# The read-out steps of a chunk moved to every second group in a selective scan kernel

## The chip, the cores and the metric

The kernel runs on one core of a Trainium2 chip. The metric is the device time of one execution in microseconds (us), from three runs of the kernel before: 1214.02, 1214.25 and 1216.48, median 1214.25.

## The reference

Two sequences of 1024 tokens with 256 channels pass through four layers with residual adds, each behind a layer norm: a selective scan (state size 64), a mixture of eight experts with two chosen for each token, a linear attention with 16 heads, and a gated feed-forward layer. The change touches only the first:

```
delta = softplus(delta @ dt_proj_w.T + dt_proj_b);  A = -exp(A_log)
step:  dA = exp(dt * A);  h = dA * h + dt * b * x;  y = einsum('bdn,bn->bd', h, c)
out = (y + x * D_param) @ out_proj_w.T
```

Here c comes from a position modulo 64, so all chunks of 64 tokens in a sequence use the same 64 rows c.

## The kernel before

The scan stage cuts the 2048 tokens into 32 chunks of T = 64 tokens and the 128 pairs of a chunk into GROUPS = 8 groups of G = 16. A list written by `scan_schedule` (line 619) gives one order of work for all engines; each engine walks the list and does its own part. For every group number gi (chunk c = gi // 8, place j = gi % 8) the entry "stream" stands for this:

- TensorE waits until the scan of group gi - 2 is done (it writes the same half of the input banks), issues `unread[gi - 1]` products that nobody reads, then 16 products with the inputs of group gi (line 927), and then 16 products with the decay exponents of group gi + 2 (line 908).
- ScalarE copies the carry of group gi - 1 into its inputs (`hand_on`, line 1094) and takes the exponential of the decays of group gi + 1 (line 1086).
- GpSimd makes the carry of group gi from the last column of the chunk before (lines 1414 and 1420) and clears the first column of its decays (line 1423).
- VectorE runs the scan of group gi - 2 (LAG = 2; line 1256), one instruction over 128 x 1024 elements, which writes h.

h has room for HS = 4 half chunks, that is two chunks: the scans of chunk c write where chunk c - 2 stood. For this a scan waits:

```
if c >= 2:
    dve.wait_ge(sem("y"), c - 1)
```

The read-out y of a chunk (lines 933 to 948) multiplies h with the rows c on TensorE: four steps j = 0 to 3, each of four matmuls (output on 32 partitions, 512 columns) into bank 6. The last of the 16 raises the semaphore "y" by one. The constant `Y_STEPS` says which steps stand in which group, counted from LAG groups after the start of the next chunk: entry 0 is place 2. After the read-out, ScalarE copies bank 6 out ("y_out", place 1 of the chunk after the next), SP moves the rows ("y_sel", place 3), and for every second chunk a tile of 128 rows is turned on TensorE ("yT", lines 976 and 981, place 5 of odd chunks), multiplied with w_out ("proj", place 1 of even chunks) and added to the residual on VectorE ("resid", line 1280).

Between these, the list spreads the preparation of later tokens ("u_" steps: for TensorE the transposes u_turn, line 993, and u_tx, line 543, and the projections u_proj, lines 999 and 1002, and u_dt, line 1011) and the router ("tr", "mm", "rank"). Those that write bank 7 may open only at certain places (`opens`, line 625): from chunk 3 on these are 1 and 3 in odd chunks and 4 and 6 in even chunks. `unread_after` (line 736) counts the other TensorE work of a group by `PE_WORK` (a read-out step and the turn count 4 each) and gives 3 less that many unread products, never below zero; they are issued at the head of the next group's stream.

Of the kernel before, what the change touches and what calls it, by code (L numbers as in the profile page):

```python
# [559 lines left out]
ZEROS = 4  # L560
CT = P // T
Y_SEL = 16 * 4
Y_STEPS = ((0,), (1,), (), (2,), (), (3,))
PE_WORK = {"y": 4, "u_turn": 4, "u_proj": 6, "u_dt": 4, "u_tx": 4, "tr": 2, "yT": 4, "proj": 4}
Y_OUT, Y_PICK = 7, 9
TILE_END = ((4, 4, "yT"), (5, 5, "yt"), (8, 6, "proj"), (8, 6, "proj2"), (10, 8, "resid"))
# [52 lines left out]
def scan_schedule():  # L619
# [46 lines left out]
    for gi in range(TOTAL + LAG):  # L666
# [13 lines left out]
        c_read -= 1  # L680
        if 0 <= c_read < CHUNKS and step < len(Y_STEPS) and Y_STEPS[step]:
            yield ("y", c_read, Y_STEPS[step])
        for at, what in ((Y_OUT, "y_out"), (Y_PICK, "y_sel")):
# [27 lines left out]
    yield from ((name, b3) for name in NORM)  # L711
    for js in (js for js in Y_STEPS if js):
        yield ("y", CHUNKS - 1, js)
# [1601 lines left out]
```

## Time and profile before

| | us |
|---|---|
| median of three runs | 1214.25 |
| profiled execution | 1212.75 |
| its span | 1211.4 |
| VectorE busy | 767.2 (63%) |
| TensorE matmul busy | 1082.1 (89%) |
| ScalarE busy | 515.0 (43%) |

The span runs from the first to the last instruction of the profiled execution. Busy time is the time in which an engine worked on an instruction; time in brackets is its share of the span. In the rows below, "idle before" in square brackets is the time in which the engine stood idle in front of the group, with the instruction that ended it. A row with x12 merges twelve instructions.

### The profile page before, as it was taken

The page shows a single profiled execution, that of the slowest core. Times are in us where ns is not written, and L with a number is a line of the kernel's source. Part 1 is how long each engine was busy: PE and PEld are TensorE (multiplying, and loading weights), DVE is VectorE, ACT ScalarE, POOL GpSimd, SP SyncE. Part 2 cuts the span into 40 slices and gives each one's busy share as a digit, 9 for nine tenths or more (in the row PEclk, how much of TensorE's full clock was granted, in tenths as well). Part 3 has the DMA queues.
Part 4 walks back from the last instruction along what each step waited for, and adds up shares of the span by engine and source line. Part 5 has one row for each costly group of instructions (what it writes and reads, how often), then busy time and mean ns, then how long its engine had stood idle before and what let it go on. Part 6 is the DMA issues. An engine that isn't in the chain of part 4 may idle for free. (4 is left out here: it accounts for less than half of the span.)

```text
span 1211.4 us, 30173 instructions
## 1 busy us (share of the span) xinstructions
PE 1082.1 (89%) x12319; PEld 729.7 (60%) x12319; DVE 767.2 (63%) x890; ACT 515.0 (43%) x1328; POOL 324.0 (27%) x949
## 2 busy tenths in 40 slices
PE   3888888888888899888878999999999899999998
PEld 2655564555545555545544777788866666576465
DVE  5999999999999999999982122111111567242111
ACT  3777676676766767656631111111112212112110
POOL 5344444343345434443242011111111210000000
PEclk9999999999999999998997999999999999999999
DMA  6767747352353434424217723232110400000000
GB/s 162 164 156 182 172 106 196 63 108 75 66 128 92 101 81 75 111 68 67 47 49 260 275 102 105 75 109 105 55 48 22 140 1 1 1 18 9 9 18 18
DMA packets 183899, 110.11 MB, mean 91 GB/s; under 512 B 95517, under 2 KB 178336, under 8 KB 181408
## 3 DMA queue, kind: packets, MB, share of 16 engines
q1 hardware_dynamic: 178816, 98.65, 31.9%
q0 software_dynamic: 3456, 8.48, 2.0%
q8 instruction: 97, 1.59, 0.6%
q10 hardware_dynamic: 1488, 1.05, 0.4%
q14 instruction: 42, 0.34, 0.1%
HBM read 63.25 MB, written 43.90 MB: 88 GB/s over the span
## 5 line engine op out<-in xcount | busy, mean ns | idle before, releaser
L1256 DVE TENSOR_TENSOR_SCAN h<-decay,psum 128x1024 f32<-128x1024 f32 x256 | 566.2, 2266 | 18.5 <-ACT psum L1094 11.0
L1086 ACT ACTIVATE decay<-psum 128x512 f32<-128x512 f32 x512 | 278.2, 596 | 47.6 <-PE psum L908 44.5
L927 PEld LDWEIGHTS psum<-xdiag,bstat 128*128 128x128 bf16 x4096 | 148.4, 99 | 122.3 <-DVE h L1256 86.7
L927 PE MATMUL psum<-xdiag,bstat 128*128 128x64 bf16 x4096 | 166.4, 195 | 22.3 <-DVE h L1256 21.1
L943 PE MATMUL psum<-h,cstat 128*32 128x512 f32 x1024 | 138.0, 613 | 3.1 <-DVE h L1256 2.1
L1583 PE MATMUL psum<-shared,hid 128*128 128x256 f32 x640 | 139.7, 379 | 0.9 <-DVE hid L1662 0.9
L1571 PE MATMUL psum<-xdt,shared 128*128 128x320 f32 (+2 forms) x512 | 139.5, 433 | 0.8 <-ACT xdt L1634 0.8
L1583 PEld LDWEIGHTS psum<-shared,hid 128*128 128x128 f32 x640 | 120.9, 190 | 17.7 <-issue 1.7
L894 PE MATMUL psum<-shared 128*128 128x512 bf16 x262 | 74.4, 391 | 60.6 <-DVE h L1256 60.6
L1571 PEld LDWEIGHTS psum<-xdt,shared 128*128 128x128 f32 x512 | 92.3, 190 | 45.2 <-issue 15.3
L908 PE MATMUL psum<-rows,shared 32*128 32x64 bf16 x4096 | 105.9, 191 | 12.4 <-DMA rows<-parts_d 8.8
L1414 POOL TENSOR_TENSOR carry<-decay,h 128x16 f32<-128x16 f32 x240 | 58.0, 242 | 208.2 <-ACT decay L1086 206.2
L2192 PE MATMUL psum<-xt,wgu 128*128 128x512 f32 x256 | 110.6, 592 | 0.0
L1695 POOL DMA_INDIRECT picked_d<-eo,to x40 | 38.9, 972 | 255.3 <-ACT eo L1631 153.0
L1662 DVE TENSOR_SCALAR hid<-psum 128x320 f32<-128x320 f32 (+1 forms) x56 | 29.1, 520 | 103.8 <-PE psum L1571 103.8
L1094 ACT COPY psum<-carry 128x16 f32<-128x16 f32 x240 | 43.3, 180 | 118.8 <-PE psum L927 99.7
L908 PEld LDWEIGHTS psum<-rows,shared 32*128 32x128 bf16 x4096 | 75.2, 94 | 27.2 <-issue 11.1
L2192 PEld LDWEIGHTS psum<-xt,wgu 128*128 128x128 f32 x256 | 48.6, 190 | 59.7 <-issue 59.5
L1665 DVE TENSOR_SCALAR eo<-psum,gate 128x256 f32<-128x256 f32 x19 | 9.2, 484 | 112.9 <-PE psum L1583 107.2
L1628 ACT ACTIVATE hid<-psum 128x320 f32<-128x320 f32 (+2 forms) x72 | 30.2, 419 | 117.7 <-PE psum L1571 117.7
L1965 DVE TENSOR_TENSOR shared<-psum,sil 128x512 f32<-128x512 f32 x32 | 22.1, 690 | 86.0 <-PE psum L2192 86.0
L1420 POOL TENSOR_TENSOR carry<-carry,u 128x16 f32<-128x16 f32 x240 | 52.9, 220 | 84.2 <-ACT u L1123 67.7
(243 smaller groups left out, 1073.4 us busy)
## 6 DMA issues: line engine op xcount, KB each, us to landing
shared<-in_w SPq DMA_DIRECT2D x16, 1024.0 KB, 4.8
xdiag<-x_parts_d SPq DMA_DIRECT2D x124, 96.0 KB
rows<-parts_d SPq DMA_DIRECT2D x128, 48.0 KB
x_parts_d<-x_parts SPq DMA_DIRECT2D x14, 384.0 KB, 3.3
x_parts_d<-x_parts SPq DMA_DIRECT2D x21, 256.0 KB, 3.2
disp_d<-r_xl SPq DMA_DIRECT2D x4, 1305.0 KB, 8.6
xd<-disp_d SPq DMA_DIRECT2D x8, 652.5 KB, 6.3
picked_d<-r_xl SPq DMA_DIRECT2D x4, 1024.0 KB, 5.4
```

The costliest lines, as they stand in the source:

```text
L894: pe.q.matmul(bank, s["astat"][:, 0, :], s["astat"][:, 0:4, :].rearrange("p c m -> p (c m)"), start=True, stop=True)
L908: ins = pe.q.matmul(bank_a[half][:, i * T:(i + 1) * T], s["astat"][strip, RCH * g + q, :], rows[strip, c % 2, q, :], start=True, stop=True)
L927: ins = pe.q.matmul(to.rearrange("p d (s e) -> p s d e", e=2), bstat[:, c % 2, b, :], xdiag[:, c % 2, b, :, d, :], start=True, stop=True)
L943: ins = pe.q.matmul(bank_y[32 * q:32 * q + 32, :].rearrange("p (s d e) -> p s d e", s=2, e=4), s["cstat"][:, tok // 4, :], h[:, first:last ...
L1086: act.q.activation(decay[:, gi % NB, 8 * half:8 * half + 8, :], per_d(bank_a[half]), ACT.Exp).then_inc(sem("exp"), 1)
L1094: act.q.copy(per_d(bank_in[gi % 2])[:, :, 0], carry[:, gi % NB, :]).then_inc(sem("handed_on"), 1)
L1256: dve.q.tensor_tensor_scan(out=h[:, half_slot(c, half), ch:ch + G, :].rearrange("p d t -> p (d t)"), data0=decay[:, gi % NB, :, :].rearran ...
L1414: pool.q.tensor_tensor(whole, first, h[:, half_slot(c - 1, half), ch:ch + G, T - 1], ALU.mult).then_inc(sem("carry_made"), 1)
L1420: pool.q.tensor_tensor(whole.rearrange("p (h i) -> p h i", h=2), whole.rearrange("p (h i) -> p h i", h=2), own, ALU.add).then_inc(sem("car ...
L1571: ins = pe.q.matmul(table.bank(key)[:, 0:cols.stop - cols.start], w1[:, e % 2, dh, f * P:(f + 1) * P], xdt[:, e % 2, dh, cols], start=dh = ...
L1583: ins = pe.q.matmul(table.bank(key)[:, 0:D], hid[:, e % 2, f, st * P:(st + 1) * P], w2[:, e % 2, f, :], start=f == 0, stop=f == FT - 1)
L2192: ins = pe.q.matmul(table.bank(key)[:, :], wgu[:, j, dh, f * P:(f + 1) * P], xt[:, u, dh, :], start=dh == 0, stop=dh == 1)
```

## The change

One constant. The four steps were at entries 0, 1, 3 and 5 of the list and are at 0, 2, 4 and 6. As places in a chunk: 2, 3, 5 and 7 of the next chunk become 2, 4 and 6 of the next chunk and 0 of the one after it. The numbers of unread products follow from it by `unread_after`.

```diff
-Y_STEPS = ((0,), (1,), (), (2,), (), (3,))
+Y_STEPS = ((0,), (), (1,), (), (2,), (), (3,))
```

## Rows read from the trace of the kernel before

**Rows 1.** Page, busy time by engine: us, share of the span, instructions.

```profile
PE 1082.1 (89%) x12319; PEld 729.7 (60%) x12319; DVE 767.2 (63%) x890; ACT 515.0 (43%) x1328; POOL 324.0 (27%) x949
```

**Rows 2.** Stretches: bounds, length, busy us of each engine, clock, DMA share, GB/s.

```profile
core 0: us, PE busy (x) PEld busy (x) DVE busy (x) ACT busy (x) POOL busy (x), PEclk, DMA share, GB/s
31.90:630.10 598.20, 510.36 (x9929) 324.76 (x9923) 583.05 (x396) 405.35 (x1098) 244.14 (x857) 0.99 0.47 105
```

**Rows 3.** Page, costliest groups: busy us, mean ns of one, idle before it.

```profile
L1256 DVE TENSOR_TENSOR_SCAN h<-decay,psum 128x1024 f32<-128x1024 f32 x256 | 566.2, 2266 | 18.5 <-ACT psum L1094 11.0
```

**Rows 4.** VectorE in order of time, chunks 6 and 7: start us, length us.

```profile
144.52 0.40 DVE L1280 TENSOR_TENSOR x1o<-psum,xres 128x256 f32<-128x256 f32 x1
144.84 26.23 DVE L1256 TENSOR_TENSOR_SCAN h<-decay,psum 128x1024 f32<-128x1024 f32 x12
171.73 8.82 DVE L1256 TENSOR_TENSOR_SCAN h<-decay,psum 128x1024 f32<-128x1024 f32 x4 [0.67 <-ACT psum L1094]
```

**Rows 5.** TensorE in order of time: one group with a read-out step, chunk 9.

```profile
193.87 6.66 DVE L1256 TENSOR_TENSOR_SCAN h<-decay,psum 128x1024 f32<-128x1024 f32 x3
196.19 0.82 PE L894 MATMUL psum<-shared 128*128 128x512 bf16 x3 [0.55 <-DVE h L1256]
196.84 0.63 PE L927 MATMUL psum<-xdiag,bstat 128*128 128x64 bf16 x16
197.41 0.41 PE L908 MATMUL psum<-rows,shared 32*128 32x64 bf16 x16
197.74 1.07 PE L943 MATMUL psum<-h,cstat 128*32 128x512 f32 x8
198.74 0.23 PE L927 MATMUL psum<-xdiag,bstat 128*128 128x64 bf16 x2
```

**Rows 6.** Order of time around the turn of a tile's rows, chunk 9.

```profile
202.62 4.44 DVE L1256 TENSOR_TENSOR_SCAN h<-decay,psum 128x1024 f32<-128x1024 f32 x2
204.32 1.07 PE L943 MATMUL psum<-h,cstat 128*32 128x512 f32 x8
205.32 0.66 PE L976 MATMUL psum<-ident,xs 128*128 128x64 f32 x4
206.76 0.63 PE L927 MATMUL psum<-xdiag,bstat 128*128 128x64 bf16 x16
207.42 0.18 ACT L1094 COPY psum<-carry 128x16 f32<-128x16 f32 x1
207.73 2.29 DVE L1256 TENSOR_TENSOR_SCAN h<-decay,psum 128x1024 f32<-128x1024 f32 x1 [0.67 <-ACT psum L1094]
```

**Rows 7.** Order of time, chunk 0: a scan that waits for matmuls alone.

```profile
40.75 0.63 PE L927 MATMUL psum<-xdiag,bstat 128*128 128x64 bf16 x16
41.48 2.29 DVE L1256 TENSOR_TENSOR_SCAN h<-decay,psum 128x1024 f32<-128x1024 f32 x1 [0.41 <-PE psum L927]
```

**Rows 8.** TensorE in order of time: unit transposes and projection, chunks 6 and 20.

```profile
148.08 0.66 PE L993 MATMUL psum<-ident,ux 128*128 128x128 f32 x4
...
152.43 1.13 PE L999 MATMUL psum<-uxn,w_proj 128*128 128x256 f32 x4
153.40 1.00 PE L1002 MATMUL psum<-w_proj,uxn 128*128 128x64 f32 x8
154.24 0.63 PE L927 MATMUL psum<-xdiag,bstat 128*128 128x64 bf16 x16
...
412.00 0.74 PE L543 MATMUL psum<-ident,ur 128*128 128x128 f32 x4
```

**Rows 9.** Waits: engine, tile, line and whom it awaited; us, times, longest.

```profile
DVE h L1256 <- ACT psum L1094: 11.0, 19, 1.0
```

**Rows 10.** VectorE in order of time, chunks 10 and 24.

```profile
230.27 1.38 DVE L1315 TENSOR_SCALAR r_xl<-x1o,r_mom,r_rstd 128x256 f32<-128x256 f32 x4 [0.93 <-ACT r_rstd L1216]
...
489.44 2.27 DVE L1256 TENSOR_TENSOR_SCAN h<-decay,psum 128x1024 f32<-128x1024 f32 x1
491.90 2.27 DVE L1256 TENSOR_TENSOR_SCAN h<-decay,psum 128x1024 f32<-128x1024 f32 x1
494.62 2.27 DVE L1256 TENSOR_TENSOR_SCAN h<-decay,psum 128x1024 f32<-128x1024 f32 x1
```

## The prediction

> **What bounds the kernel now.** The first view to read is the page's list of busy time [rows 1]: it names TensorE first (89%), and that is the average of two stages. The stretches [rows 2] divide it. The scan stage takes 598.2 of the 1211.4 us, and in it VectorE is busy for 583.05 us: 256 scans of about 2.27 us [rows 3] hold it. The rest of the kernel does not know the changed list, so I expect it to move as a block with the end of the scan stage.
>
> Then VectorE alone in order of time [rows 4]. Twelve scans take 26.23 us, which is (26.23 - 2.27) / 11 = 2.18 us from one start to the next; the row runs across the starts of chunks 6 and 7 with no gap. So in a quiet stretch the stage advances by one scan in 2.18 us, and what counts is only what makes a scan start later than that. The same rows show two such things: the 0.40 us residual add on VectorE itself in even chunks, and a wait of 0.67 us once in an odd chunk. I call the place of a group in its chunk 0 to 7.
>
> A group without a gap, seen from TensorE [rows 5]: the scan before starts at 193.87 + 2.19 = 196.06, and TensorE, which waited for the scan ahead of that, starts at 196.19, 0.13 later. Then come the unread products (0.65 us until the inputs start), the inputs (0.57), the decays of the group after next (0.33), and a read-out step (1.00 until the next group's inputs; its end is shown 1.07 after its start). That is 2.55 us, more than one scan, and still no scan is late: the next group has no unread products and catches up. A scan needs its inputs only 0.97 us after they start (206.76 to 207.73, through the copy of the carry at 207.42) [rows 6]. So a group in which TensorE is occupied for w delays the scan of the next group by 0.13 + w + 0.97 - 4.36 if that is above zero, 4.36 being two scans. For the turn of a tile's rows with a read-out in front of it, w = 0.65 + 0.57 + 0.33 + 1.00 + 1.44 = 3.99 and the delay 0.73; measured it is 207.73 - 204.80 - 2.18 = 0.75 [rows 6].
>
> **The change, part by part.** Read-out step j stands at places 2, 3, 5, 7 of the chunk after its own; afterwards at 2, 4, 6 and at 0 of the chunk after that. No instruction is added or taken away but unread products: they are three less a group's other work, are issued at the head of the next group, and a read-out leaves none.
>
> The turn (place 5 of odd chunks) loses the read-out. Group 4 is then the 2.55 us one, group 5 takes 0.57 + 0.33 + 1.44 = 2.34; together 0.13 + 4.89 + 0.97 = 5.99 against the 6.54 of three scans: no wait is left. Ten of the fifteen turns show the 0.75 (chunks 5, 7, 9, 11, 13, 19, 21, 23, 27 and 29); chunks 3, 17 and 25 show 0.54, 0.53 and 0.43; in 15 and 31 VectorE's own small work covers it. Sum 9.0. Chunk 3 also loses a read-out beside a projection, 0.3. Gain 9.3 us. All waits of scans for the carry's copy sum to 11.0 us over 19 places [rows 9], which bounds this gain at about 11.0 + 19 x 0.08 = 12.5 (a start after a wait also loses the overlap of two scans, 2.26 - 2.18); below, it is bounded by zero.
>
> The fourth step at place 0. The scan of the first group of chunk c + 2 overwrites the rows of h that the read-out of chunk c reads, and waits until the semaphore "y" says that chunk c is read. Before, the last step stood one group earlier and that wait was long met. Now it is issued in the very group whose scan waits for it, behind that group's inputs and the decays. And place 7, emptied of its read-out, leaves three unread products, which stand at the head of place 0. By [rows 5]: 0.13 + 0.65 + 0.57 + 0.33 + 1.07 = 2.75 us from the start of the scan before to the end of the read-out, and 0.10 from a matmul's shown end to a scan that waits for it (41.38 to 41.48) [rows 7]. So the scan starts 2.85 after the one before instead of 2.18: 0.67 us held, with nothing else on VectorE to fill it. Queued behind it on VectorE are all later scans and the router's operations, so each hold moves the rest of the stage; ScalarE's copy of bank y comes at place 1, after that moment in any case, and TensorE goes on at once, so nothing is given back later. It happens at the starts of chunks 2 to 31, 30 times. Twenty-one of these stand in unbroken rows (0.66 to 0.67 each, 14.0). At chunks 16, 19, 26 and 27 small operations leave 0.60, 0.40, 0.53 and 0.11 (1.6). At 11, 17, 25, 28 and 31 the two intervals ahead of the start are already over 5.03 (494.62 - 489.44 = 5.18 at chunk 25 [rows 10]) and hide it. Sum 15.6 us. Bounds: zero, if the hold were hidden; 0.9 each (+6) if carry or exponentials come late as well.
>
> The Trainium skill (Perfetto Trace Analysis, Tensor Engine Instruction) says that a matmul's end in a profile is computed from its size and that the semaphore follows later, when the bank has acknowledged. The trace agrees: 0.10 us in [rows 7]. By the shown ends alone, without it, the holds would sum to 13.1 instead of 15.6.
>
> Places 4 and 6 of even chunks. These are the places at which the units' transposes and projections open in even chunks, and there was no read-out there. Eleven groups at place 4 (chunks 4, 6, 8, ... 24) have transposes of 0.66 or 0.74 us [rows 8], some 0.6 and 0.67 occupied: w = 0.65 + 0.57 + 0.33 + 0.67 + 1.00 = 3.22, and 0.13 + 3.22 + 0.97 = 4.32, just under 4.36. I take nothing, and 0.3 each (3.3) as the upper bound. Five at place 6 (chunks 6, 10, 14, 18, 22) have the unit's projection, 154.24 - 152.43 = 1.81 [rows 8]: w = 4.36, delay 0.13 + 4.36 + 0.97 - 4.36 = 1.10. That is 3.3 in chunks 6, 14 and 22. In chunk 18 the batch statistics make the scan late anyway. In chunk 10 the projection stands ahead of the router's reciprocal deviation on ScalarE, for which VectorE already waits 0.93 us [rows 10]; I put 0.4 there. Two router transposes with a logit product (chunks 12 and 28) reach 4.56, 0.2 for the one that is not covered. Sum 3.9, bounds 0 and 8.
>
> SP's queue keeps its order; its copies out of the read rows wait for ScalarE's copy at place 1, which may end some 0.6 us later, and the turn that needs them comes four groups on. The unread products that leave places 3 and 6 and come at 4, 6 and 0 are in the sums above.
>
> **The sum.** -9.3 + 15.6 + 3.9 = +10.2 us on the profiled execution's 1212.75 (its span is 1211.4), so 1222.9. The three runs shown have a median of 1214.25, 1.5 above the profiled one; the prediction for such runs is 1214.25 + 10.2 = 1224.4.
>
> **The rivals.** First, crowded even chunks tip over: all eleven transposes wait 0.3 and the projections drag their copies along. For it: 0.04 us of margin. Against: ScalarE still has slack there. 1224.4 + 5 = 1229.5. Chance 0.16.
>
> Second, the turn is not relieved, since group 4 now arrives late in front of it: 1224.4 + 9.3 = 1233.7. Against it the margin of 6.54 - 5.99 = 0.55. Chance 0.07.
>
> Third, the hold is half covered. TensorE is let go by the scan before last, so every delay of the scan at place 7 gives it the same lead on place 0, as at chunk 25. If the read-out at place 6, new there too, makes that scan late in many chunks, the two waits share their time: 15.6 / 2 = 7.8, hence 1214.25 - 9.3 + 7.8 + 3.9 = 1216.7. Against it: 0.13 + 2.55 + 0.97 = 3.65 leaves the scan after a plain read-out group 0.7 us of room. Chance 0.09.
>
> Fourth, on the other side: the last step ends before the scan in front does, the hold is nil, and the relief of the turn wins: 1214.25 - 9.3 + 3.9 = 1208.9, or 1205 if the projections are covered too. It decides at one point: whether inputs, decays and read-out of place 0 end within 2.18 - 0.10 us after the scan in front starts. Without the unread products they would take 2.10 and it would be near; with them 2.75. Chance 0.06. That the change doesn't do what it says, because other work fills the turn's group, is in the second: its place 5 stays in no other list.
>
> **How the numbers follow.** The forecast has 0.62, its own range 1220 to 1228. With the third and first case taken in, the range that should hold 8 in 10 is 1217 to 1231. A change under 0.2% (2.4 us) could not be told from none. Faster comes from the fourth case: 0.06. Same: 0.03, from the low end of the third. Slower: 0.91.
>
> **What the profile after would show.** In the list of waits, scans of h waiting for the read-out's matmul (none today) about 25 times, near 0.6 us of idle each; VectorE's row broken at each chunk start, in eight scans instead of twelve. No wait at place 6 of odd chunks after the turn. One wait above 1 us at place 7 of chunks 6, 14 and 22. The stage after the scans as long as before. The prediction is wrong if scans cross the chunk starts unbroken, or if the 0.67 us at the turn stays.

## The result and the profile after

The changed kernel takes 1232.74 us (median of four runs, 1229.15 to 1233.6) against 1214.13 for the kernel before (four runs, 1213.65 to 1216.48): ratio 1.0141, 95% interval 1.0115 to 1.0167. It is 18.6 us slower; 10.2 were forecast, and 1232.7 lies above the range, whose upper end was 1231.

The page's line of the scans, and the two waits of scans that matter, from the list of waits (us in total, times, longest):

```profile
L1256 DVE TENSOR_TENSOR_SCAN h<-decay,psum 128x1024 f32<-128x1024 f32 x256 | 568.1, 2269 | 35.6 <-PE psum L943 15.9
```

```profile
DVE h L1256 <- PE psum L943: 15.9, 23, 2.2
DVE h L1256 <- ACT psum L1094: 11.2, 12, 1.5
```

A scan itself takes as long as before (2269 ns against 2266 in [rows 3]), but VectorE's idle in front of scans has gone from 18.5 to 35.6 us. The first wait did not exist: scans wait for the read-out's matmul, 23 times. The second was 11.0 us in 19 places [rows 9]; it is as large, in fewer places, and so it is not the same wait any more.

VectorE in order of time, chunks 6 to 9 (start, length, idle before):

```profile
147.35 0.40 DVE L1280 TENSOR_TENSOR x1o<-psum,xres 128x256 f32<-128x256 f32 x1
147.66 10.99 DVE L1256 TENSOR_TENSOR_SCAN h<-decay,psum 128x1024 f32<-128x1024 f32 x5
159.79 2.29 DVE L1256 TENSOR_TENSOR_SCAN h<-decay,psum 128x1024 f32<-128x1024 f32 x1 [1.14 <-ACT psum L1094]
162.56 17.53 DVE L1256 TENSOR_TENSOR_SCAN h<-decay,psum 128x1024 f32<-128x1024 f32 x8 [0.48 <-PE psum L943]
180.76 4.47 DVE L1256 TENSOR_TENSOR_SCAN h<-decay,psum 128x1024 f32<-128x1024 f32 x2 [0.67 <-PE psum L943]
185.15 0.40 DVE L1280 TENSOR_TENSOR x1o<-psum,xres 128x256 f32<-128x256 f32 x1
185.46 6.72 DVE L1256 TENSOR_TENSOR_SCAN h<-decay,psum 128x1024 f32<-128x1024 f32 x3
193.40 6.64 DVE L1256 TENSOR_TENSOR_SCAN h<-decay,psum 128x1024 f32<-128x1024 f32 x3 [1.22 <-ACT psum L1094]
```

Three of the forecast's steps can be read here. The row of x8 at 162.56 is the whole of chunk 7, from its held first scan through the turn without a gap: the 0.67 us of [rows 4] at the turn are gone. At 180.76 the first scan of chunk 8 is held. At 159.79 a scan waits for the crowded group with the projection at place 6 of chunk 6. The last row is one that was not foreseen: 1.22 us at place 5 of chunk 8.

The hold, close up (chunk 9 into 10):

```profile
193.40 6.64 DVE L1256 TENSOR_TENSOR_SCAN h<-decay,psum 128x1024 f32<-128x1024 f32 x3 [1.22 <-ACT psum L1094]
197.92 0.82 PE L894 MATMUL psum<-shared 128*128 128x512 bf16 x3 [0.88 <-DVE h L1256]
198.58 0.63 PE L927 MATMUL psum<-xdiag,bstat 128*128 128x64 bf16 x16
199.15 0.40 PE L908 MATMUL psum<-rows,shared 32*128 32x64 bf16 x16
199.48 1.06 PE L943 MATMUL psum<-h,cstat 128*32 128x512 f32 x8
200.71 4.46 DVE L1256 TENSOR_TENSOR_SCAN h<-decay,psum 128x1024 f32<-128x1024 f32 x2 [0.67 <-POOL decay L1423]
```

The scan in front starts at 193.40 + 2 x 2.19 = 197.78; unread products, inputs, decays and the fourth step stand between it and the next, as forecast, and end at 200.54. The scan starts 0.17 us later, not 0.10. This row names GpSimd's clearing of a decay column as the releaser, since one ended 0.07 us before the scan. In 28 of the 30 chunk starts the scan begins 0.16 to 0.18 us after the shown end of the read-out, whether a clearing ended 0.02 or 1.60 us before it, so the read-out is what it waits for in this one too.

Now the surprise, chunk 8, in four stretches (length, busy us of TensorE's matmuls, weight loads, VectorE, ScalarE, GpSimd, then the granted clock as a share of 2.4 GHz, DMA share, GB/s):

```profile
182.00:185.30 3.30, 2.56 (x44) 1.15 (x42) 3.30 (x3) 1.90 (x5) 0.59 (x4) 1.00 0.49 137
185.30:188.40 3.10, 1.57 (x35) 1.10 (x36) 3.10 (x3) 1.26 (x3) 2.29 (x7) 1.00 0.33 98
188.40:191.80 3.40, 3.40 (x42) 2.27 (x43) 3.40 (x2) 1.85 (x5) 0.43 (x2) 0.50 1.02 319
191.80:195.00 3.20, 3.15 (x75) 1.94 (x67) 1.98 (x2) 2.35 (x6) 0.47 (x4) 1.00 0.93 315
```

TensorE ran at 1.2 GHz from 188.4 to 191.8, right after 3.10 us in which it was busy for 1.57. The trace in order of time says what stood there:

```profile
185.29 0.64 PE L927 MATMUL psum<-xdiag,bstat 128*128 128x64 bf16 x16 [0.21 <-DVE h L1256]
185.86 0.41 PE L908 MATMUL psum<-rows,shared 32*128 32x64 bf16 x16
187.80 0.90 PE L894 MATMUL psum<-shared 128*128 128x512 bf16 x3 [1.53 <-DVE h L1256]
188.49 1.06 PE L927 MATMUL psum<-xdiag,bstat 128*128 128x64 bf16 x16
191.07 1.42 PE L943 MATMUL psum<-h,cstat 128*32 128x512 f32 x8
```

Place 3 is now a light group, nothing but inputs and decays, and it follows a read-out, so that no unread products stand at its head either. In even chunks the residual add delays the scan in front by 0.3 more. TensorE idles 1.53 us, and the next group, the one with transposes and a read-out, meets the lower clock: its inputs take 1.06 us instead of 0.63, and its read-out 1.42, of which only a part lies in the slow stretch. In the trace of before, the scan stage has four such episodes after its first microseconds (17 us in all), all of them behind VectorE's router work. After, there are nine (37 us), in chunks 5, 8, 10, 15, 19, 20, 24, 28 and 30. Six of them (5, 8, 10, 20, 24, 30) follow an idle of TensorE of 1.53 or 1.60 us behind a light group, with no router work in front of it. The one of chunk 15 follows 1.39 us; those of chunks 19 and 28 stand behind router work as before, after 2.56 and 4.88 us. An idle of this length is not enough by itself: behind its first chunk the stage has 22 of more than 1.3 us where the kernel before had 7, and 13 of the 22 pass without a fall. What decides between them is not shown.

The Trainium skill (TensorE: Matmul & The Clock Gate, HAM oscillation — how this bites in real kernels) describes a kernel with waits between its bursts of matmuls, whose clock falls in each wait. The trace agrees that the clock falls behind such waits, but not on their length: they are longer there, and in chunk 8 no idle of the matmuls was above 1.53 us. The measurement decides.

Where the 19.8 us of the scan stage lie, from one scan's start to the next, summed by place over all chunks (us more than before, each rounded; the last column is experiment e3, below):

| interval | forecast | changed | e3 |
|---|---|---|---|
| place 7 to 0 (the hold) | +15.6 | +19.0 | +17.3 |
| 5 to 6 (the turn) | -9.0 | -9.8 | -9.8 |
| 6 to 7 (projection) | +3.9 | +2.4 | +2.9 |
| 4 to 5 | 0 | +6.6 | +1.4 |
| the rest | -0.3 | +1.6 | -1.3 |
| sum | +10.2 | +19.8 | +10.5 |

The stages around it differ by 1.1 us between the two spans.

### The profile page after: what moved, and what is told of

Same layout as the page of the kernel before. It is cut to its first block and busy times, and to the rows that moved or that the text cites. A ratio compares the mean times of both kernels' runs of the same rounds, so it can differ in the third digit from the quotient of the medians.

```text
span 1232.3 us, 30157 instructions
## 1 busy us (share of the span) xinstructions
PE 1088.3 (88%) x12311; PEld 727.6 (59%) x12311; DVE 769.1 (62%) x890; ACT 511.7 (42%) x1328; POOL 324.0 (26%) x949
## 5 line engine op out<-in xcount | busy, mean ns | idle before, releaser
L1256 DVE TENSOR_TENSOR_SCAN h<-decay,psum 128x1024 f32<-128x1024 f32 x256 | 568.1, 2269 | 35.6 <-PE psum L943 15.9
L943 PE MATMUL psum<-h,cstat 128*32 128x512 f32 x1024 | 141.5, 628 | 2.1 <-DVE h L1256 1.8
L894 PEld LDWEIGHTS psum<-shared 128*128 128x128 bf16 x254 | 18.4, 99 | 98.8 <-DVE h L1256 85.9
```

The costliest lines, as they stand in the source:

```text
L894: pe.q.matmul(bank, s["astat"][:, 0, :], s["astat"][:, 0:4, :].rearrange("p c m -> p (c m)"), start=True, stop=True)
L943: ins = pe.q.matmul(bank_y[32 * q:32 * q + 32, :].rearrange("p (s d e) -> p s d e", s=2, e=4), s["cstat"][:, tok // 4, :], h[:, first:last ...
L1256: dve.q.tensor_tensor_scan(out=h[:, half_slot(c, half), ch:ch + G, :].rearrange("p d t -> p (d t)"), data0=decay[:, gi % NB, :, :].rearran ...
```

## The experiments

Theory H: the scan of place 0 is held by the read-out issued in its own group. Theory C: what exceeds the forecast is TensorE's clock, which the light groups let fall. The rivals: the excess comes from the transposes and the read-out in one group; or the holds are longer than they look.

**e1, the fourth step back at place 7.**

```diff
-Y_STEPS = ((0,), (), (1,), (), (2,), (), (3,))
+Y_STEPS = ((0,), (), (1,), (), (2,), (3,))
```

> The changed kernel with the last read-out step alone put back to place 7 (steps at 2, 4, 6, 7). Theory H (the scan of place 0 waits for the read-out issued in its own group, 0.75 us start to start): the 23 waits of scans for L943 go, some 18 us of the place 7 to place 0 intervals; at place 7 a group of 2.5 us now follows the projection group of 3 chunks (+1). About 1215 us. Rival C (it is the clock: more stretches at 1.2 GHz, whatever waits for what): the places 3 and 5 stay light groups, the number of half-clock stretches in the scan stage stays near nine and the time stays above 1225.

Ratio to before 0.9974 (0.9953 to 0.9995), some 1211 us on the scale of the case. No scan waits for L943 any more, and the interval 7 to 0 is at -0.6 us against before. The stage stands at +3.0. H holds. Half-clock stretches remain (seven in the stage after its first chunk), at other places: the time fell all the same, so the rival in its strong form falls.

**e2, no unread products at the head of place 0.**

```diff
-    return [max(0, 3 - w) for w in work]
+    return [0 if gi % GROUPS == GROUPS - 1 else max(0, 3 - w) for gi, w in enumerate(work)]
```

> The changed kernel without the three unread products at the head of place 0. Theory H: the read-out of place 0 ends 0.65 us earlier, so each of some 25 holds shrinks from 0.75 to about 0.1: -16 us, about 1216. Rival C: the products kept the clock up, and without them more stretches run at 1.2 GHz, each of which costs 1 to 2 us where a read-out falls into it: more than the 10 stretches of now and less than 10 us gained.

1.0052 (1.0030 to 1.0074): against the 1.0141 of the changed kernel 11 us less, not 16. The wait of scans for the read-out, from the list of waits:

```profile
DVE h L1256 <- PE psum L943: 2.7, 7, 0.5
```

From 15.9 us to 2.7: the products were the larger part of the hold. In the stage the interval 7 to 0 gives back 14.7 us, near the 16 expected. But the trace has ten stretches at half clock in the stage, one more than the changed kernel, the interval 3 to 4 takes 1.8 us more, and the interval 4 to 5 keeps its +6.4 us. H holds, and what it doesn't explain is still there.

**e3, unread products in the light groups.** Each group without work of its own that follows a group with one step of work gets three:

```diff
-    return [max(0, 3 - w) for w in work]
+    return [3 if w == PE_WORK["y"] and not after else max(0, 3 - w) for w, after in zip(work, work[1:] + [1])]
```

> The changed kernel with three unread products more at the head of each group that has no work of its own and follows a group with one step of work (places 1, 3, 5, 7 for the most part). Theory C (after a light group of 0.9 us of matmuls TensorE idles 1.5 us and the granted clock falls to 1.2 GHz at the next group; the extra 8 to 9 us over the forecast are these stretches): the stretches at 1.2 GHz fall from ten to about three (those behind VectorE's router work), and the time by 7 to 9 us, to about 1224; the holds of 0.75 stay. Rival (the extra comes from the transposes and the read-out standing in one group at place 4): no stretch matters, chunks 8, 20 and 24 keep their 1.3 to 1.5 us, the time stays at 1232 or rises by the added products.

1.0096 (1.0072 to 1.0119). In the profiled execution the nine stretches at half clock in the stage are one (chunk 28, behind router work), and the stage stands at +10.5 us. The same stretches of time around chunk 8:

```profile
185.30:188.40 3.10, 2.22 (x58) 1.59 (x55) 3.10 (x2) 1.47 (x5) 1.33 (x4) 1.00 0.43 121
188.40:191.80 3.40, 3.02 (x50) 1.77 (x52) 3.40 (x3) 3.19 (x7) 0.59 (x3) 1.00 1.01 313
```

and VectorE and TensorE there in order of time:

```profile
184.36 11.01 DVE L1256 TENSOR_TENSOR_SCAN h<-decay,psum 128x1024 f32<-128x1024 f32 x5
184.41 0.59 PE L894 MATMUL psum<-shared 128*128 128x512 bf16 x2 [0.43 <-DVE h L1256]
186.69 0.82 PE L894 MATMUL psum<-shared 128*128 128x512 bf16 x3 [0.88 <-DVE h L1256]
188.25 0.74 PE L543 MATMUL psum<-ident,ur 128*128 128x128 f32 x4
188.93 1.06 PE L943 MATMUL psum<-h,cstat 128*32 128x512 f32 x8
```

The clock stays at 2.4 GHz, five scans run on without a gap, and the group with transposes and a read-out costs nothing: this is the same group that held 1.22 us in the changed kernel. That rules out the rival of the crowded place 4: a group with more work in front is faster.

The two traces can be laid side by side, interval by interval. They differ by more than 0.6 us in eight intervals only. Seven of these overlap a half-clock stretch of the changed kernel (in chunks 5, 8, 15, 19, 20, 24 and 30) and sum to 8.3 us; that shows C. The eighth, 1.6 us in chunk 28, ends before the clock falls there and is no matter of the clock: VectorE waits for a DMA that reads the tile it is about to write, 1.72 us in the changed kernel and 0.13 in e3.

```profile
574.53 1.38 DVE L1315 TENSOR_SCALAR r_xl<-x1o,r_mom,r_rstd 128x256 f32<-128x256 f32 x4 [1.72 <-DMA disp_d<-r_xl,slots]
```

The times are less clear than the trace. The profiled execution of e3 took 1223.1 us, its other three 1227.4 to 1229.3, at mean granted clocks of 0.979 to 0.990 against its 0.983. What those three lost is not shown. By the ratios e3 is only 5.5 us faster than the changed kernel, and the two intervals touch.

**e4, the turn freed and nothing at place 0.** The kernel before, with other steps only where they fall into odd chunks:

```diff
+Y_TURN = ((0,), (1,), (), (), (2,), (3,))
...
+        steps = Y_STEPS if c_read % 2 else Y_TURN
```

> The kernel before with one difference: where the read-out falls into an odd chunk (the one with the turn at place 5) the steps stand at 2, 3, 6 and 7 instead of 2, 3, 5 and 7; even chunks as before. So the turn has its own group, no step stands at place 0 and none shares a group with an even chunk's transposes. Theory H and the sum for the turn: the 0.75 us at place 5 to 6 go in ten odd chunks, 9.0 to 9.7 us in all, and nothing comes in their place: about 1205. Rival: the read-outs at 6 and 7 in a row make the first scan of the next chunk late (two groups of 2.55 us less 4.36), giving back up to 0.3 a chunk: 1209 or more; or new half-clock stretches after places 4: 1209 or more as well, told apart by the clock.

0.9909 (0.9883 to 0.9936), about 1203 on the scale of the case, slightly better than expected. The stage of the profiled execution, the slowest of its four, stands at -5.3: -5.9 at the turn, since long stretches at half clock (10.2 us each, in chunks 10 and 19) took some of it back. The idea of the change was right; its place 0 was not.

**e5, the changed kernel again**, beside e6 to e8.

> The changed kernel itself, timed beside the next three. Ratio to before 1.014 again. Theory C expects the stretches at 1.2 GHz to lie again at places 3 and 4 of even chunks for the most part, perhaps in other chunks, since they come and go; the rival (they belong to chunks 8, 20 and 24 because of the transposes there) expects the same chunks.

1.0162 (1.0125 to 1.0198), stage +21.2. The stretches at half clock number twelve, in chunks 5, 8, 10, 14, 15, 20, 22, 24, 26, 28, 30 and 31; eight of them begin at place 3 of an even chunk. Eight chunks are those of the first trace, among them 8, 20 and 24; 14, 22, 26 and 31 are new, and 19 has none. Chunks 26 and 30 have no unit's transposes, so a fall doesn't need them.

**e6, steps at 2, 4, 6, 7 with unread products in the light groups** (the edits of e1 and e3).

> Steps at 2, 4, 6, 7 (no hold at place 0) and unread products in the light groups. Without holds and without half-clock stretches there stay the turn's gain of 9 to 10 us and the crowded place 6 of 3 to 4 us: theories H and C together give the kernel before less 5 to 6 us, ratio 0.995, with at most three half-clock stretches in the scan stage after its first chunk. If C is wrong it stays at the 0.9974 of the run without the products.

0.9989 (0.9966 to 1.0012). A miss by 0.4%: stage -0.9 us, not -5 to -6. Two stretches at half clock are left, as forecast, but the products take their own toll: +3.5 us in the interval 7 to 0, 0.6 each in chunks 6, 12, 14, 22 and 28. There three of them stand at the head of place 0, behind the crowded place 6 and the read-out at place 7; in e1, without them, the same five intervals are as before. Against e1 (0.9974) nothing is gained.

**e7, e4 with unread products in the light groups.**

> The kernel before with the steps of odd chunks at 2, 3, 6, 7, and unread products in the light groups. Theory C: the stretches at 1.2 GHz of the version without the products (5 in the scan stage) fall to one or two and the time by 3 to 4 us more, to a ratio of 0.988 (the turn's 9 us, the clock's 4, less what the products cost). Rival: the products stand ahead of inputs on the path and cost what they bring: 0.991 as without them.

0.9949 (0.9926 to 0.9973): a miss, with both the 0.988 of theory C and the 0.991 of the rival below the interval. The profiled stage stands at -8.6 us, with all of -9.1 at the turn and two stretches at half clock. As the ratio goes it is no better than e4's 0.9909, which was timed on another chip; the two were not timed side by side, and which is faster stays open. Both beat the kernel before.

**e8, no products at place 0, and products in the light groups**, with the changed places.

```diff
+    return [0 if gi % GROUPS == GROUPS - 1 else 3 if w == PE_WORK["y"] and not after else max(0, 3 - w)
+            for gi, (w, after) in enumerate(zip(work, work[1:] + [1]))]
```

> The changed places 2, 4, 6, 0, with no unread products at the head of place 0 and three in the light groups. Theory H: the hold shrinks to 0.1 to 0.2 at some 25 chunk starts, and with the clock kept up the stage is that of the kernel before + 10.5 - 17.25 + 4 = -3 us: ratio 0.998, against 1.005 without the products in light groups and 1.010 with the products at place 0. Rival: the hold stays (the wait is for something else than the end of the fourth step): 1.009.

1.0035 (1.0014 to 1.0056), a miss above the expected 0.998; stage +1.4 us for -3, two stretches at half clock (the list of waits; an added line moves the numbers by one):

```profile
DVE h L1257 <- PE psum L944: 5.6, 13, 0.5
```

In eight chunk starts the hold falls from 0.75 to 0.16, as expected, in twelve only to 0.43 to 0.57. Five of the twelve (the starts of chunks 7, 13, 15, 23 and 29) stand behind a crowded place 6, which makes the fourth step late as well. The added products have no part in them: e2, which has none in light groups, shows the same 0.57 in all five. Its trace and that of e8 at the start of chunk 7:

```profile
159.15 6.64 DVE L1256 TENSOR_TENSOR_SCAN h<-decay,psum 128x1024 f32<-128x1024 f32 x3 [0.46 <-PE psum L943]
```

```profile
160.80 4.46 DVE L1257 TENSOR_TENSOR_SCAN h<-decay,psum 128x1024 f32<-128x1024 f32 x2 [0.46 <-PE psum L944]
```

Three more (chunks 2, 5 and 9) were at 0.10 in e2; in e8 products stand at the heads of both place 6 and place 7 in front of them. That these cost the rest was not tested, and for the last four (6, 10, 20 and 22) I have no reading. H holds; my figure for the rest of the hold was too small.

**e9, the kernel before with unread products in the light groups.**

> The kernel before with unread products in the light groups as well, nothing moved. Control for theory C: its four half-clock stretches in the scan stage lie behind VectorE's router work, not behind light groups, so the added products have little to repair: 0 to -3 us, ratio 0.998 to 1.000. Rival: the products help any version by 8 to 10 us, whatever the read-out's places, and the excess of the changed kernel is no matter of its places: 0.993.

1.0008 (0.9986 to 1.0031). The stage stands at -0.8 us, with two stretches at half clock instead of four. The products do nothing that can be measured in the time for the places of before, which keeps C to the changed places: what e3 repairs is what the change had broken.

**e10 and e11, the change in odd chunks alone and in even chunks alone.**

```diff
+Y_MOVED = ((0,), (), (1,), (), (2,), (), (3,))
...
+        steps = Y_STEPS if c_read % 2 else Y_MOVED        # e10;  "if not c_read % 2" in e11
```

> Read-outs that fall into odd chunks stand at 2, 4, 6 and at 0 of the even chunk after; those in even chunks stay at 2, 3, 5, 7. Theory H: holds of 0.75 at the starts of even chunks alone (about 12 full ones, 9 us), the turn's -9.7, no crowded place 6: stage 0 to +1 us. Theory C in the form that the fall comes at the light place 3 of even chunks, behind the residual add: few half-clock stretches beyond those of before. Ratio 1.000. Rival: the stretches come from the alternation in any chunk: 5 or more extra, ratio 1.004.

> The other half: read-outs that fall into even chunks stand at 2, 4, 6 and at 0 of the odd chunk after; odd chunks as before. Theory H: holds of 0.75 at the starts of odd chunks (about 12, 9 us), crowded place 6 (3.5), the turn's waits stay. Theory C: the half-clock stretches of the changed kernel at places 3 and 4 of even chunks are all here, 5 or more of them with 1.0 to 1.5 us each where a read-out falls in: 6 us. Stage +18 to +20 us, ratio 1.015 to 1.017. Rival: without them +12.5, ratio 1.010.

e10 is 1.0002 (0.9980 to 1.0024): 12 waits of 0.67 and less for the read-out, -10.0 us at the turn, +11.1 at the interval 7 to 0, stage -0.2, with six stretches at half clock, two more than before. e11 is 1.0109 (1.0074 to 1.0145): holds at the starts of odd chunks, the crowded place 6 at +2.6, and the turn's waits as before; stage +11.1. The waits of e10 and then of e11 (numbers moved by two):

```profile
DVE h L1258 <- PE psum L945: 7.9, 12, 0.7
```

```profile
DVE h L1258 <- PE psum L945: 5.7, 10, 0.7
DVE h L1258 <- ACT psum L1096: 14.4, 19, 1.4
```

For e11 the rival was right: five stretches at half clock, not five more, and +11 instead of +18 to +20. My version of C for e11, that the fall belongs to place 3 of even chunks alone, is too narrow: e11 has 23 idles of the matmuls over 1.3 us, no fewer than the changed kernel's 22, and five falls where that had nine. In the profiled executions the halves sum to -0.2 + 11.1 = +10.9 us, where the whole has +19.8 and +21.2, as if the excess of 9 to 10 us belonged to neither half and needed both kinds of chunks. The ratios don't bear that out beyond the noise: the halves make 1.0111, give or take 0.004, and the whole 1.0141 and 1.0162. It stays open.

## Why the prediction was wrong

What held. The turn's waits are gone, at -9.8 us for the -9.0 forecast. The hold is there, in the group, by the wait and in the chunks named. The projection's groups at place 6 of chunks 6, 14 and 22 show 1.22 us each for 1.10. The transposes at place 4 cost nothing at full clock (e3), for all that the margin was 0.04 us. The forecast's likeliest mechanism and its sign were right. That e3's stage stands at +10.5 and the two halves sum to +10.9, for +10.2, is closer than the terms are: in e3 the hold is 1.7 us over its term and the interval 4 to 5 1.4 over, and 0.8 at the turn, 1.0 at the projection and 1.0 in the rest are under. The errors cancel, and that is luck. Part of it is that e3 lacks half-clock stretches that the kernel before had, as the one of chunk 19, where it is 1.4 us shorter.

What failed, first and by far: the sentence that the unread products "are in the sums above". It counted them as time ahead of the inputs and put at nothing, without a word, what their absence does to the clock. Every term was worked out at 2.4 GHz, from the rows of before. The alternation of 2.55 us groups and 0.9 us groups left TensorE's matmuls idle for 1.5 to 1.6 us behind light groups, and the clock fell to 1.2 GHz nine times instead of four, six of them behind such an idle. At that clock a whole read-out takes 1.94 us for 1.06 (the row below, chunk 5 of the changed kernel), and a group that just fitted doesn't. The changed kernel's stage is 9.3 us longer than e3's: 5.2 in the intervals 4 to 5, 1.7 in 7 to 0 (most of it 1.55 at the end of chunk 15, where the hold lies in such a stretch), and the rest elsewhere. Of this 8.3 us lie in intervals with half-clock stretches; 1.6 are the DMA wait of chunk 28. This compares one execution of each, and the ratios give 5.5 us. No rival had it: the nearest, crowded even chunks that tip over, named the right groups and the wrong reason, and e3 refutes the reason.

```profile
128.43 1.94 PE L943 MATMUL psum<-h,cstat 128*32 128x512 f32 x8
```

Second, and small: the hold is 0.75 us, start to start, instead of 0.67. The read-out's semaphore reaches VectorE 0.17 us after the shown end, where the inputs' takes 0.10 [rows 7]; 23 x 0.07 = 1.6 us. The prediction knew that a matmul's shown end is computed, and then took the delay of another form of matmul for this one.

The range of 1217 to 1231 was too narrow on the slow side, by 1.7 us, for the first reason: its upper end was built from terms at full clock.

## What to carry to other kernels

When a change moves work on TensorE, list the idle time that it leaves in each step of the new order, beside the work: the falls of the clock cost 8 us here in the profiled execution, nearly as much as the rest of the change. A step that frees a buffer should not be issued in the group whose scan writes it; one group earlier it cost nothing (e1). And where a rearrangement helps one kind of iteration only, it should be made there only: e4 and e7 free the turn in odd chunks alone, and they are the fastest versions here.

## What the runs showed of the hardware that was not expected

TensorE's granted clock fell to 1.2 GHz in chunk 8 with no idle of the matmuls longer than 1.53 us (1.57 us of them in the 3.10 before), and with unread products of 0.65 us in the light groups (e3) it stayed at 2.4 GHz through the stage behind its first chunk but for one stretch. A matmul's semaphore acts at different delays behind its shown end: 0.10 to 0.11 us for the bf16 inputs of 64 columns, 0.16 to 0.18 for the float read-out of 512.
